# Moving the third head pair's value products behind the next batch's second key chunk in a gated cross-attention block

## The reference

```python
# per batch; 8 heads of 64
xn = layernorm(ctx, gm, bm); ln = layernorm(_layernorm(x), gl, bl)
q = ln @ Wq                                   # 224 queries
k, v = split(concat([xn, ln]) @ Wkv)          # 974 keys and values
sim = (q / scale) @ k.T                       # per head
out = softmax(sim - max(sim)) @ v
x = x + tanh(g_xattn) * (out @ Wout)
h = square(relu(_layernorm(x) @ W_fc.T)); y = h @ W_proj.T
x = x + tanh(g_ffn) * spikes(y, 5 steps) / 5
```

## Time and profile before

| | |
|---|---|
| median of three runs | 1051.58 us |
| span of the profiled execution (first to last instruction) | 1050.2 us |
| TensorE matmul busy | 1032.4 us, 98% |
| VectorE busy | 792.4 us, 75% |
| ScalarE busy | 593.0 us, 56% |
| GpSimd busy | 314.6 us, 30% |
| mean granted TensorE clock | 0.998 of full |

### The profile page before, as it was taken

One profiled execution on the slowest core, in us unless ns is written; L12 is line 12 of the kernel. 1 busy time (PEld: TensorE's weight loads), 2 busy tenths in 40 slices (PEclk: granted clock), 3 DMA queues, 4 the chain that ended last, 5 costly groups with the idle time before them and its releaser, 6 DMA issues.

```text
span 1050.2 us, 19053 instructions
## 1 busy us (share of the span) xinstructions
PE 1032.4 (98%) x6940; PEld 842.3 (80%) x6940; DVE 792.4 (75%) x1228; ACT 593.0 (56%) x1147; POOL 314.6 (30%) x289
## 2 busy tenths in 40 slices
PE   5999999999999999999999999999999999999997
PEld 4878778877877877887787787777788888998887
DVE  6488879987987987998798798779434555585766
ACT  6558547656654854765665485467446433455435
POOL 5333633335434363333543436334000000000000
PEclk9999999999999999999999999999999999999999
DMA  6302010100201201010020200122530000201011
GB/s 196 135 1 75 5 36 23 53 6 28 76 0 35 75 1 35 23 53 8 27 76 0 75 0 0 35 86 58 157 120 21 1 1 29 93 2 41 21 61 42
DMA packets 31907, 47.43 MB, mean 45 GB/s; under 512 B 2300, under 2 KB 11532, under 8 KB 31868
## 3 DMA queue, kind: packets, MB, share of 16 engines
q1 hardware_dynamic: 31732, 46.74, 13.8%
q10 hardware_dynamic: 136, 0.17, 0.1%
HBM read 39.56 MB, written 7.34 MB: 45 GB/s over the span
## 4 chain that ended last, share of the span: by engine, by line
PE 96%; DVE 2%; DMA 1%; ACT 1%; issue 0%; SPq 0%; DVEq 0%; ACTq 0%
PE work L491 42%; PE work L644 14%; PE score L657 13%; PE heads_out L596 9%; PE score L570 9%; PE score L506 2%; PE heads_out L608 1%; PE score L861 1%; DMA vals<-in_L_xattn_Wkv 1%; PE maxes L583 1%; PE heads_out L491 1%; DVE on L1457 0%; PE maxes L578 0%; PE maxes L596 0%; PE score L777 0%
## 5 line engine op out<-in xcount | busy, mean ns | idle before, releaser
L1882 POOL TENSOR_TENSOR dsum<-dsum,probs 125x448 f32<-125x448 f32 x186 | 221.1, 1189 | 14.6
L491 PE MATMUL work<-wv,xT 128*125 128x512 f32 (+1 forms) x768 | 187.0, 397 | 0.0
L491 PE MATMUL work<-xT,wk 128*128 128x486 f32 (+2 forms) x756 | 181.7, 390 | 1.5 <-DVE xT L1506 1.0
L491 PEld LDWEIGHTS work<-wv,xT 128*125 128x125 f32 (+1 forms) x768 | 137.9, 183 | 37.4 <-issue 2.3
L644 PE MATMUL work<-zT,wf 128*128 128x512 f32 (+1 forms) x768 | 164.1, 364 | 0.0
L491 PEld LDWEIGHTS work<-xT,wk 128*128 128x128 f32 x756 | 137.9, 188 | 31.0 <-issue 4.6
L644 PEld LDWEIGHTS work<-zT,wf 128*128 128x128 f32 x768 | 131.5, 189 | 23.0 <-issue 0.7
L999 ACT ACTIVATE probs<-score 125x448 f32<-125x448 f32 (+1 forms) x256 | 119.8, 548 | 46.2 <-PE score L570 46.2
L1879 POOL TENSOR_TENSOR dsum<-probs 125x448 f32<-125x448 f32 x31 | 41.0, 1322 | 340.2 <-ACT probs L1005 340.2
L1410 DVE TENSOR_TENSOR probs<-probs,maxes 125x1792 f32<-125x1792 f32 x64 | 128.4, 2016 | 1.1
L657 PE MATMUL score<-hT,wp 128*128 128x512 f32 (+1 forms) x576 | 117.4, 354 | 0.0
(11 more groups left out here) (207 smaller groups left out, 1447.8 us busy)
## 6 DMA issues: line engine op xcount, KB each, us to landing
xin<-in_ctx SPq DMA_DIRECT2D x42, 250.0 KB
neuron<-in_L_ffn_W_fc SPq DMA_DIRECT2D x16, 256.0 KB, 3.1
neuron<-in_L_ffn_W_proj SPq DMA_DIRECT2D x16, 256.0 KB, 3.0
xres<-in_x SPq DMA_DIRECT2D x16, 224.0 KB, 2.6
x_scratch<-xres SPq DMA_DIRECT2D x16, 224.0 KB, 2.5
xin<-in_x SPq DMA_DIRECT2D x14, 224.0 KB, 9.9
zt<-x_scratch SPq DMA_DIRECT2D x3, 1024.0 KB, 6.5
fin<-x_scratch SPq DMA_DIRECT2D x3, 1024.0 KB, 5.7
```

The source lines that it names most:

```text
L491: mm = pe.matmul(bank, lhs(i, k), rhs(j, k), start=(n == 0), stop=(n == len(passes) * chunks - 1))
L1882: pool.tensor_tensor(total[0:ROWS[t]], total[0:ROWS[t]], tile(t), ALU.add).then_inc(dchain if t < TILES - 1 else dsum_done, 1)
```

## The change

One call moves behind four others, and one moves ahead of one. Everything is in TensorE's loop body; the last batch's own order, and the other engines' orders, stay.

```diff
                 totals(b, 1)
                 keys_queries(b + 1, 0, (2,))
                 keys_queries(b + 1, 1, (0,))
-                attend(b, 2)
                 keys_queries(b + 1, 1, (1,))
                 max_transposes(b, 3)
                 keys_queries(b + 1, 1, (2,))
                 max_rows(b, 3)
+                attend(b, 2)
+                totals(b, 2)
                 scores(b + 1, 0, 0)
-                totals(b, 2)
                 keys_queries(b + 1, 2, (0, 1))
                 scores(b + 1, 0, 1)
                 attend(b, 3)
```

## The result

The changed kernel takes 1059.5 us (median of four runs, 1059.05 to 1059.75) against 1051.45 us (1051.04 to 1052.86) in the same session: a ratio of 1.0074 with a 95% interval of 1.0063 to 1.0086. That is 8.0 us slower; 1059.9 was predicted, in a range of 1056.5 to 1062.6. The interval of the ratio is 6.6 to 9.0 us, so the runs alone can't tell 8.0 from the 7.3 us by which the span of the profiled execution grew (1050.2 to 1057.5 us). The time lies 1.8 us above the span, in the kernel before as well: in its 45 executions beside the experiments and in the four of the changed kernel it is 1.76 to 1.87 us. The 1.4 us named ahead of the prediction are a median less the span of an execution whose own time isn't known.

What follows compares the result with a forecast made beforehand. TensorE, working without a pause inside the loop, was taken to bound the kernel. Seven iterations at 1.19 us more add 8.3 to the 1050.2 us span, giving 1058.5; plus 1.4 makes 1059.9 us, range 1056.5 to 1062.6.

Steps and rivals of the forecast that it cites:

- Steps 1, 3 and 4: TensorE's four stages come 3.18 us forward; max_transposes waits for maxima until about 286.31; queries wait for the bank, losing 1.16 us.
- rival B: VectorE frees the bank 1.2 us or more ahead of 286.89, so 0.35 us less in all, 1051.2; chance 0.04.
- Step 2: TensorE's second key half waits for VectorE's low part of pair 0's queries: 0.04 us lost, not adding to the next wait.
- Steps 5 and 7: Restart after the wait costs 0.08 us, queries take 1.50; max_rows to value products 0.32, value products 3.08, totals 0.48, scores 1.50.
- Step 8: TensorE's summed stretch ends at 293.82, not 292.63: 1.19 us more; fewer changes between kinds of product give back 0.05 at most.
- Step 6: max_rows on TensorE needs query_maxima, ready at about 288.0, 0.4 us ahead: no loss, but the thinnest cover left.
- Steps 9 and 10: Later in the iteration nothing is won back or lost; each of seven iterations pays 1.19 us, 8.3 us together.
- One sentence of the opening: Until its 1.86 us pause VectorE works through a backlog, so the moved stages' new places can't make it earlier.
- Rival D: TensorE's clock falls to 1.2 GHz after each gap and 6.9 us of work takes twice as long: about 1108; chance 0.01.

Runs made afterwards that it cites:

- exchange of the two stages: Changed kernel with VectorE's low part of the first key half, which frees the bank, put ahead of maxima: 1059.11 us.
- the smaller move: Kernel before with the value products moved behind the second key half only, totals left in place: 1052.22 us, ratio 1.0007.
- The run with short sums and a short normalise: Changed kernel with GpSimd's denominators of pair 2 and VectorE's normalise of pair 1 cut to 8 of 224 columns: 1052.86 us.
- both reorderings: Changed kernel with VectorE's normalise and heads_lo of pair 1 moved back, 1071.58 us; the same with max_rows behind value products and totals, 1064.11 us.
- the run with more VectorE work: Changed kernel with an additional VectorE reciprocal of 1.55 us in each iteration: 1072.46 us; the same addition in the kernel before: 1051.46 us.
- the run with VectorE's order mended: Changed kernel with normalise of pair 1 behind maxima and the first low part, heads_lo and ScalarE's heads_hi further back: 1071.58 us.

## Why the prediction was right, by its own steps
Steps 1, 3 and 4, that the late partner is VectorE and that the bank wait ends last: shown. With the first key products of pair 1 as zero, the queries start at 289.13 - 282.39 = 6.74 us; predicted were 286.94 - 280.23 = 6.71. The low part that frees the bank ends 289.08 - 282.39 = 6.69 us behind that zero, before it was 286.89 - 280.23 = 6.66: VectorE came no earlier, and rival B is out. More work on VectorE costs only in the changed kernel, and less work there brings time back. The exchange of the two stages supports this less, since its equal time is a balance. The rows of the waits were forecast at about 0.5 and 0.6 us and are listed at 0.37 and 0.36; by starts the second is 0.60 as forecast, and the first, together with the wait inside the key products, 0.78 against a forecast 0.56.

Step 2, the wait for the queries' low part: it is there, at the weight loads, and the next wait swallowed it, as said. Where nothing swallows it, it costs about 0.14 us and not 0.04, as the smaller move showed.

Steps 5 and 7, restart and neighbours: mis-sized, both upwards. The queries take 290.57 - 289.13 = 1.44 us and not 1.50. From max_rows to the value products it is 290.80 - 290.57 = 0.23 and not 0.32: the 0.32 of the earlier trace rows has a max_rows whose weight load itself came late, with 0.28 us idle ahead of it, and the 0.23 that I kept as the other bound was right. Value products 3.08, totals 0.48 and scores 1.49 came as read. The list gives 13.46 in place of 13.59, so 1.06 us; another 0.03 to 0.04 is won just behind it, where the next key products and scores take 302.81 - 295.85 = 6.96 us against 7.00. That is 1.03 against the predicted 1.19, 7.2 against 8.3 over seven iterations.

Step 8, what the new order gives back: mis-sized, 0.05 us at most was predicted. The run with short sums and a short normalise has the changed kernel's order on TensorE with about 0.60 us of waiting, and takes 293.21 - 280.53 = 12.68 us where the kernel before takes 12.40. Without that wait it would be about 12.08, 0.3 us less than before. This is an estimate from those rows, and no run had this order without a wait. The difference is in the two key products in a row (5.33 us up to max_transposes, and 5.52 where scores follow, from which step 2 took its 2.76), in the value products (3.08 in place of 3.18) and in the totals (0.48 in place of 0.52). So waits and restart cost about 1.40 us in place of 1.24, the order gives back over 0.3 us in place of 0.05, and a part of the agreement is luck. It also bears on the remark that nothing here could take 0.3 us off an iteration: this order without its waits would come close to it.

The total of 1059.9 came nearer to 1059.5 than its parts, and that too is luck: the span was forecast at 1058.5 and is 1057.5, while the runs lie 1.8 us above it and not 1.4.

Step 6: right, max_rows doesn't wait. L1393 ends at 290.15, 0.42 us ahead of it. That cover was as thin as said: in the run with the keys first max_rows did come 0.2 us late.

Steps 9 and 10: right. No further wait, nothing is given back, and the seven iterations are alike.

One sentence of the opening needs a limit. VectorE has a backlog there, but a short one: ScalarE's part of the queries ends only 0.6 us ahead of VectorE's (L1033 at 283.66 + 0.45 = 284.11, L1427 at 284.71). I took the chain for one that could be moved 1.9 us by reordering, in the experiments and not in the prediction, and both reorderings failed on it, the first also because it put normalise ahead of what max_rows needs.

Rival D, the clock, had 0.01. For the changed kernel it didn't come: its gaps of 0.37 and 0.36 us stand at the full clock in all seven iterations. But the two windows of the earlier trace rows were thin support for 0.01. Gaps of 1.6 and 0.35 us had a fall to the 1.2 GHz level behind them in three of seven iterations, gaps of 0.63, 0.36 and 0.88 us in three of seven, and gaps of 0.36 and 0.87 us in one of seven. The Trainium skill's "TensorE: Matmul & The Clock Gate", section "A second HAM failure mode: psum-queue depth-cycling", tells of a kernel that idles briefly and often between groups of matmuls while the clock goes back and forth; these three traces agree, the changed kernel's doesn't show it. A fall cost 1.6 us in the run with more VectorE work, a fourth of the 6.9 us that I priced, and 3.2 us in the longest case (the first iteration of the run with VectorE's order mended).

## What to carry to other kernels
When an engine works without a pause, read the slack of every stage that a move brings forward, to the end of the last operation it waits for: 3.18 us forward against a slack of 2.07 gave the loss to 0.2 us, with the help of two smaller errors that cancelled in part. Work that looks movable may be cover for another engine's chain, and it needs to stand ahead of the stages that this chain feeds. A listed wait can understate its cost, so compare starts with a stretch that has no wait. Before moving a late chain forward by taking work out of it, look for the next input that it would wait for.

## Not expected of the hardware
- A VectorE operation with two inputs in memory (128x448, the first step of pair 3's maxima) took 0.61, 0.84 or 1.40 us, depending on where it met GpSimd's sums. With the sums of pair 2 cut short it took 0.62 to 0.63 in every iteration. So moving work to another phase can gain or lose 0.2 to 0.8 us by this alone.
- Idle stretches of TensorE well under 2 us had a fall of its granted clock to 0.50 behind them, but not each time: 1.62 and 0.35 us in three of seven iterations, 0.36 and 0.87 us in one of seven, 0.37 and 0.36 us in none of the seven in the changed kernel's trace.
